# Expert blocks of 64 rows, two side by side on the halves of a product, in place of blocks of 128 rows

## The reference

```python
logits = flat @ router_w.T
scores = jax.nn.softmax(logits, axis=-1)
_, topk_idx = jax.lax.top_k(logits + router_bias, TOPK)          # TOPK = 2
...
for e in range(N_EXPERTS):                                       # 16
    h = jax.nn.silu(flat @ Wu[e]) * (flat @ Wg[e])               # 256 -> 128, twice
    out = out + combine[:, e:e + 1] * (h @ Wd[e])                # 128 -> 256
for s in range(N_SHARED):
    out = out + jax.nn.silu(flat @ Su[s]) * (flat @ Sg[s]) @ Sd[s]
...
x = x + jnp.tanh(g_ffn[0]) * _L0_ffn_ref(_layernorm(x, axis=-1), ...)
```

## Time and profile before

| | |
|---|---|
| median of 3 runs | 438.38 us (436.29 to 438.97) |
| the profiled execution's own time | 438.61 us |
| its span, first to last instruction | 436.8 us |
| mean granted clock of TensorE over the span | 0.969 of 2.4 GHz |
| PE busy over the span | 387.8 us (89%) |
| DVE / ACT / POOL busy | 352.9 / 294.6 / 278.0 us |
| blocks: first to last product of experts | about 369 to 418 us of the span |

### The profile page before, as it was taken

How to read it: one execution, slowest core, us unless ns; L and a number is a source line. 1 busy time by engine, 2 the same in 40 slices (tenths; PEclk the granted TensorE clock), 3 DMA queues, 4 the chain that set the end, 5 groups by cost and what they waited for, 6 DMA issues and landing times.

```text
span 436.8 us, 11224 instructions
## 1 busy us (share of the span) xinstructions
PE 387.8 (89%) x3626; PEld 288.6 (66%) x3626; DVE 352.9 (81%) x804; ACT 294.6 (67%) x621; POOL 278.0 (64%) x379
## 2 busy tenths in 40 slices
PE   0577799999999999999999999999998497999970
PEld 0445567667667767676766777676687286999960
DVE  5867979999999998999999999999889762334336
ACT  2598788777877777876877787787973315666510
POOL 2068866886787687688588677765574750366650
PEclk9999999999999999999999999999989688999995
DMA  8960868999980000000000000000194213444308
GB/s 209 261 228 2 106 90 259 253 287 286 243 230 3 0 0 0 0 0 0 0 0 0 0 0 0 0 2 2 33 434 194 96 67 98 124 132 136 99 22 277
DMA packets 34621, 45.57 MB, mean 104 GB/s; under 512 B 2970, under 2 KB 32031, under 8 KB 33696
## 3 DMA queue, kind: packets, MB, share of 16 engines
q1 hardware_dynamic: 26368, 35.34, 27.4%
q0 software_dynamic: 6944, 9.46, 9.9%
q10 hardware_dynamic: 1280, 0.41, 0.5%
HBM read 28.21 MB, written 24.19 MB: 120 GB/s over the span
## 4 chain that ended last, share of the span: by engine, by line
PE 73%; DVE 11%; ACT 4%; DMA 4%; issue 3%; POOL 3%; POOLq 0%; ACTq 0%; SPq 0%; DVEq 0%
PE proj_ps L972 18%; PE proj_ps L964 8%; PE score_ps L1001 8%; PE pv_ps L1024 8%; PE headT_ps L990 6%; PE out_ps L1034 6%; PE proj_ps L1138 4%; PE headT_ps L1138 3%; PE score_ps L990 3%; PE probT_ps L1010 3%; DMA cenf<-in_cen 2%; PE score_ps L1153 1%; DVE xs L1702 1%; DVE arena L1326 1%; PE pv_ps L1153 1%
## 5 line engine op out<-in xcount | busy, mean ns | idle before, releaser
L972 PE MATMUL proj_ps<-arena 128*128 128x512 f16 x384 | 100.0, 383 | 3.0 <-DVE arena L1356 3.0
L1364 DVE BATCH_NORM_STATS2 st<-rot 128x6 f32<-128x256 f32 x192 | 72.6, 419 | 10.6 <-ACT rot L710 10.0
L572 POOL TENSOR_TENSOR rot<-rot,cw 128x512 f32<-128x512 f32 x64 | 77.9, 1238 | 2.5
L710 ACT ACTIVATE rot<-proj_ps 128x512 f32<-128x512 f32 x96 | 56.1, 585 | 7.6 <-PE proj_ps L972 6.0
L972 PEld LDWEIGHTS proj_ps<-arena 128*128 (+1 forms) x384 | 32.5, 98 | 32.3 <-issue 3.8
L642 POOL DMA_INDIRECT ybuf<-arena,bslot x31 | 30.5, 984 | 31.3 <-DVE bslot L1612 14.6
L731 ACT ACTIVATE rot<-rot,cw 128x128 f32<-128x128 f32 x128 | 40.9, 391 | 11.0 <-POOL cw L566 10.4
L578 POOL TENSOR_TENSOR reg<-reg,rinv 128x512 f32<-128x512 f32 x32 | 33.4, 1044 | 21.9 <-DVE rinv L1374 21.9
L964 PE MATMUL proj_ps<-arena 128*128 128x512 f16 x192 | 46.7, 379 | 0.6 <-POOL arena L528 0.6
L1024 PEld LDWEIGHTS pv_ps<-reg,vv 64*128 64x128 f32 x512 | 31.1, 187 | 12.9 <-issue 9.7
L990 PE MATMUL headT_ps<-idf,rot 128*128 128x128 f32 x256 | 38.5, 273 | 0.1
(11 more groups left out here) (229 smaller groups left out, 850.2 us busy)
## 6 DMA issues: line engine op xcount, KB each, us to landing
zbuf<-fill SPq DMA_DIRECT2D x1, 16576.5 KB, 65.5
arena<-in_wffn SPq DMA_DIRECT2D x4, 1536.0 KB, 13.4
arena<-zbuf SPq DMA_DIRECT2D x30, 128.5 KB, 2.2
wkv_stage<-in_wkvN SPq DMA_DIRECT2D x1, 2048.0 KB, 15.4
wp_sb<-in_wpT POOLq DMA_DIRECT2D x1, 2048.0 KB, 16.4
wp_sb<-ybuf SPq DMA_DIRECT2D x8, 256.0 KB, 4.5
xs<-in_x SPq DMA_DIRECT2D x2, 512.0 KB, 5.5
vv<-in_wqN POOLq DMA_DIRECT2D x1, 1024.0 KB, 12.5
```

The lines of the kernel that those rows point to most:

```text
L572: gp.tensor_tensor(r, r, cw[:, 4 * i:4 * i + 4].unsqueeze(2).to_broadcast([P, 4, D]), ALU.mult)\
L710: act.activation(raw[c % 2][i], proj_ps[i % 2][:, :], ACT.Copy).then_inc(proj_evac, 1)
L972: mm = pe.matmul(ps, lhs, w[kind][:, ch, 512 * b:512 * b + 512], start=(k == 0), stop=(k == 3))
L1364: ins = ve.bn_stats(st[:, 4 * i + h:4 * i + h + 2, :].rearrange("p h s -> p (h s)"), raw[c % 2][i][:, h * D:(h + 2) * D].rearrange("p (h d ...
```

## The change

Blocks have 64 rows (`BR`). At most 47 exist; 48 are worked, four at a time in 12 steps: two in the lower 64 partitions of `zb`, two in the upper. In the product the 64 rows of tokens are stationary and occupy one half of the array's columns; 256 numbers of the weights move (up and gate side by side). The lower half takes its weights from `wall` at a register's place, the upper half takes them from a copy, `wfix`, that DVE and ACT make, one block each and all 768 numbers (three buffers, a wait on `down_done`). The result has the rows on the partitions, so the gated rows `hid` are transposed by PE (`hidden_transposes`, two more transposes), copied out by ACT (`hidden_out`), and are stationary for `block_down`, again in halves. SP reads four beginnings and issues four transfers of 64 rows for each step. POOL's scatters stay at 128 rows, two for each step. The table on DVE compares with 16 numbers for each expert instead of 8.

```diff
-NBLK = 31
-NPAIR = (NBLK + 1) // 2
+NBLK = 48
+NPAIR = NBLK // 4
...
-                for b in (range(1) if s == 0 else parts(s)):
-                    sp.dma_start(zb[s % 3][:, b, :], zbuf[bass.ds(base[b], P), :]).then_inc(zb_ld[s % 3], 16)
-                base = [sp.value_load(bbase[j:j + 1, 0:1], min_val=0, max_val=SLOTS)
-                        for j in range(2 * s + 2, min(2 * s + 4, NBLK))]
+                for j in range(2 if s == 0 else 4):
+                    half = slice(j % 2 * BR, (j % 2 + 1) * BR)
+                    sp.dma_start(zb[s % 3][half, j // 2, :], zbuf[bass.ds(base[j], BR), :]).then_inc(zb_ld[s % 3], 16)
+                if s + 1 < NPAIR:
+                    base = [sp.value_load(bbase[j:j + 1, 0:1], min_val=0, max_val=SLOTS)
+                            for j in range(4 * s + 4, 4 * s + 8)]
...
             def block_weights(s):
-                for b in parts(s):
-                    ins = act.activation(wup[s % 2][:, b, :], wall[:, bass.ds(base[b], 2 * H)], ACT.Copy)
+                if s >= 3:
+                    act.wait_ge(down_done, FIRST + s - 2)
+                act.activation(wfix[s % 3][:, 1, :], wall[:, bass.ds(base, WE)], ACT.Copy).then_inc(wfix_act, 1)
+            def hidden_out(s):
+                act.wait_ge(hidT_done, s + 1)
+                ge(act, down_done, FIRST + s - 1)
+                act.activation(hidT[s % 2], hidT_ps[s % 2][:, 0:2 * P].rearrange("p (b t) -> p b t", b=2),
+                               ACT.Copy).then_inc(hidT_evac, 1)
...
+            for s in range(NPAIR):
+                unit_silu(FIRST + s)
+                if s + 2 < NPAIR:
+                    block_rows(s + 2)
+                hidden_out(s)
+                if s + 2 < NPAIR:
+                    block_weights(s + 2)
...
+            def block_up(s, base):
...
+                for b in range(2):
+                    o = slice(b * 2 * P, (b + 1) * 2 * P)
+                    for c in range(HC):
+                        pe.matmul(up_ps[u % 2][0:BR, o], zTb[s % 2][:, b, c, 0:BR],
+                                  wall[:, bass.ds(base[b] + 2 * c * P, 2 * P)], start=(c == 0), stop=(c == HC - 1))
+                        mm = pe.matmul(up_ps[u % 2][BR:P, o], zTb[s % 2][:, b, c, BR:P],
+                                       wfix[s % 3][:, b, 2 * c * P:2 * (c + 1) * P], start=(c == 0), stop=(c == HC - 1))
+            def hidden_transposes(s):
+                pe.wait_ge(hid_done, u + 1)
+                ge(pe, hidT_evac, s - 1)
+                for b in range(2):
+                    mm = pe.transpose(hidT_ps[s % 2][:, b * P:(b + 1) * P], hid[u % 2][:, b * P:(b + 1) * P], idf[:, :])
...
-            for u in range(FIRST, end):
-                if u + 1 < end:
-                    bases[u + 1] = offsets(u + 1 - FIRST)
-                    block_up(u + 1)
-                if u - FIRST + 2 < NPAIR:
-                    block_transposes(u - FIRST + 2)
-                unit_down(u, bases[u])
+            block_up(0, base)
+            block_transposes(2)
+            hidden_transposes(0)
+            for s in range(NPAIR):
+                if s + 1 < NPAIR:
+                    following = offsets(s + 1)
+                    block_up(s + 1, following)
+                block_down(s, base)
+                base = following
+                if s + 3 < NPAIR:
+                    block_transposes(s + 3)
+                if s + 1 < NPAIR:
+                    hidden_transposes(s + 1)
...
+            def block_weights(s):
+                base = NSH * WE + ve.value_load(bbase[4 * s + 1:4 * s + 2, 1:2], min_val=0, max_val=(NE - 1) * WE)
+                if s >= 3:
+                    ve.wait_ge(down_done, FIRST + s - 2)
+                ve.tensor_copy(wfix[s % 3][:, 0, :], wall[:, bass.ds(base, WE)]).then_inc(wfix_dve, 1)
```

More of the change, by code:

```diff
@@ L102, in shared_tile, with scattered_back @@
     return u if u < FIRST else u - NPAIR if u >= FIRST + NPAIR else None
[L105 to L112, removed]
 def landed(s):
-    return 16 * sum(len(parts(r)) for r in range(s % 3, s + 1, 3))
+    return 64 * (s // 3 + 1)
+def scattered_back(s):
+    return 32 * (s // 3 + 1)
 def run_steps(eng, step, between={}):
@@ L265, in build @@
         zT = xT
-        wup = [qT[:, i, :, :].rearrange("p h t -> p (h t)").rearrange("p (b o) -> p b o", b=2) for i in range(2)]
+        hidT = [qT[:, i, 0:2, :] for i in range(2)]
+        wfix = [a[:, 0:2 * WE].rearrange("p (b o) -> p b o", b=2)
+                for a in (reg1, reg2, vv[:, :, :].rearrange("p a t -> p (a t)"))]
         yg = wp[:, :, :].rearrange("p h o -> p (h o)").bitcast(F32).rearrange("p (t k d) -> p t k d", t=NT, k=TOPK)
@@ L883, in _ @@
             act.wait_ge(table_done, 1)
[L884 removed]
+            base = [act.value_load(bbase[j:j + 1, 0:1], min_val=0, max_val=SLOTS) for j in (2, 3)]
             act.wait_ge(fill_done, 16)
             act.wait_ge(scattered, 16 * NT * TOPK)
[L887 removed]
+            for j in range(2):
+                act.dma_start(zb[0][j * BR:(j + 1) * BR, 1, :], zbuf[bass.ds(base[j], BR), :]).then_inc(zb_ld[0], 16)
             for i in range(1, 5):
                 act.wait_ge(ld_we[i], 16)
[L890 to L893, removed]
+            for s in range(2):
+                block_rows(s)
+                block_weights(s)
+            for s in range(NPAIR):
[5 more added lines that the diff above has]
+                    block_weights(s + 2)
+            for u in range(FIRST + NPAIR, NUNIT):
                 unit_silu(u)
[L895 to L897 removed]
         @block.tensor
@@ L1146, in unit_down @@
                     pe.wait_ge(y_done, NU * NT)
-                for b in parts_of(u):
+                for b in range(2):
                     h = hid[u % 2][:, b * P:(b + 1) * P]
[L1149 to L1154, removed]
+                    mm = pe.matmul(down_ps[u % 2][:, 0:H], h, wall[:, base[b] + 2 * H:base[b] + 3 * H],
+                                   start=(b == 0), stop=(b == 1))
                 mm.then_inc(down_done, 1)
@@ L1231, in _ @@
             pe.wait_ge(table_done, 1)
-            bases = {FIRST: offsets(0)}
+            base = offsets(0)
             for i in range(1, 5):
@@ L1487, in _ @@
             iota = rowv[:, NE:2 * NE]
-            full = rowv[:, 2 * NE:2 * NE + 8]
+            full = rowv[:, 2 * NE:2 * NE + NSTEP]
             block_no, block_row = rowv[:, NROWV - 2:NROWV - 1], rowv[:, NROWV - 1:NROWV]
@@ L1680, in _ @@
             route_weights()
-            unit_hidden(FIRST)
             unit_out(FIRST - 1)
             end = FIRST + NPAIR
-            row_places(0)
-            row_places(1)
-            for u in range(FIRST + 1, end - 1):
-                unit_out(u - 1)
-                unit_hidden(u)
-                row_places(u - FIRST + 1)
-            unit_hidden(end - 1)
-            unit_out(end - 2)
+            ve.wait_ge(table_done, 1)
+            for i in range(1, 5):
+                ve.wait_ge(ld_we[i], 16)
+            for s in range(2):
+                block_weights(s)
+                row_places(s)
+            for s in range(NPAIR):
+                unit_hidden(FIRST + s)
+                if s > 0:
+                    unit_out(FIRST + s - 1)
+                if s + 2 < NPAIR:
+                    block_weights(s + 2)
+                    row_places(s + 2)
             unit_out(end - 1)
```

85 lines of the change are left out of this document (48 added, 37 removed).

## The result

The changed kernel takes 455.97 us (median of 4 runs, 455.06 to 457.39), the kernel before beside it 437.71 (4 runs, 436.29 to 438.97): 1.0421 times as long, 95% interval 1.0376 to 1.0466, 18 us slower. The profiled execution took 456.06 us, its span is 454.2. The direction was predicted; 456 lies outside the range of 441 to 454, and the size was forecast at half of what it is.

A forecast was written before the change was run, and what follows sets the result against it. The prediction took PE's array as the bound before and its sequencer's loop, 4.63 us a step, after. The last scatter would land at 432.6 instead of 424.12, +8.5 on 438.6: 447 us, range 441 to 454.

The forecast's parts named there:

- SP's transfer: SP's queue in each step: 0.52 us for each of four transfers; with four loads, 4.3 us a step.
- the loop: PE's sequencer, from one up product's start to the next: offset loads queue behind the `hid` wait, 4.63 us a step.
- SP binds above the loop: Rival on SP's queue: its issues come slower, its step is 5.0 us, total 451 us; chance 0.15.
- The sign that the prediction gave for this rival: SP in the profile after: no wait behind its four transfers and four loads would mean SP is the bound, 451 us.
- Up(1) starts: Start of the blocks: after up(0) at 371.7 and hidden transposes at 374.8, the second up product starts at 376.5.
- if only in the first steps, 449: Rival on TensorE's clock: 1.2 GHz after idle gaps, only in the first steps, 449 us; all or part, chance 0.06.
- The tail: From the start of up(11) at 422.8 to the last scatter's landing at 432.6, with no POOL backlog.
- The halves: Expert products on PE: both array halves run at the same time, up 1.74 us and down 0.87 a step.
- the rival by which they show: Rival on PE's weight loads: not hidden under running products, 1.1 us a step, total 460 us; chance 0.02.
- A change of shape: PE's array, changing into halves and back: one such change a step, 0.14 us, giving 3.41 us of array time.
- DVE's copy: DVE's copy of 768 weights for the upper half: about 1.0 us, at the start ahead of up(0).
- the array rival: Rival with PE's array as bound: offset loads read ahead, cheaper SP transfers, steps of 3.41 us, total 433.5 us; chance 0.07.

The follow-up runs named there:

- e10_rows63: The changed kernel with blocks of 63 rows in place of 64: 449.92 us, 1.0259 times the kernel before.
- e5_before64: The kernel before with each transfer of 128 rows split into two of 64: 453.79 us, 1.0306 times the kernel before.
- e2_hoist: The changed kernel with PE's two offset loads moved ahead of the row transposes and the wait for `hid`: 455.21 us, 1.0341 times the kernel before.
- e1_static: The changed kernel with the 48 block beginnings written as constants, so SP does no register loads: 450.62 us, 1.0250 times the kernel before.
- e3_both: The changed kernel with the edits of e1_static and e2_hoist together: 438.10 us, 0.9962 times the kernel before.
- e9_before63: The kernel before with each transfer of 128 rows split into 63 and 65 rows: 446.17 us, 1.0172 times the kernel before.

## Why the prediction missed, step by step

**The step that failed is SP's transfer.** The prediction said: "A transfer of 64 rows may cost less to issue than one of 128; the bounds are 0 to 0.52". It cost more: 0.66 us from one to the next, where 0.52 was both my value and my upper bound. Four of them are 0.56 us over, and with four loads the turn is 4.94 instead of 4.3. Of the rest, up to the mean of 5.28, the chain shows single long instructions (a transfer of 1.06 at 409.23, loads of 0.45 to 0.52). That put SP above the loop of 4.5, and made the rival "SP binds above the loop" true, with a dearer step than its 5.0. Bounding the unknown from below alone was the error: the nearest row was one shape, and nothing in it excluded a higher price for another. The sign that the prediction gave for this rival, four loads with no wait behind them, is what the chain shows. That it is the issue time, and not the loads' count, is shown by e10_rows63, in which only the row count and so the issue time changes much: its ten steps from up(1) to up(11) take 425.23 - 379.81 = 45.4 us, where the kernel after needs 52.6. e5_before64 shows the same price in the other kernel.

**How the 8.8 us come about.** The last scatter has landed at 439.30 + 2.12 = 441.42, forecast 432.6.
- Up(1) starts at 378.50, forecast 376.5: +2.0. The granted clock was 0.50 of 2.4 GHz, its lower level, from 366 to 374; ahead of that PE had been busy for 0.93 us of the 2 from 362 to 364 and for none of the 2 from 364 to 366. The passes of up(0) lie 0.43 us apart instead of 0.217, 1.7 us in all. The prediction had this as a case, "if only in the first steps, 449".
- The loop: had all ten steps been as short as the quick ones, 4.53, they would make -1.0.
- The ten steps took 431.11 - 378.50 = 52.6 instead of 45.3: +7.3. The whole of it goes with SP's price, since e10_rows63 has none of it; but not all of it is SP's mean turn. 2.8 lie in one step (from 388.1 to 395.5), whose four transfers were issued from 387.04 to 389.50 and let the transposes start only at 393.62, 4.6 us after the start of the last issue (389.03) where 2.1 to 2.7 is usual. e2_hoist has its longest step, 6.90, at the same transfers (387.3 to 389.3), one of which took 4.0 us to land there, so this is no accident of one execution; why they land late isn't settled. Of the other steps those above the loop have 0.2 to 1.8 more each. In that with 1.8, up(9) began after an idle stretch at 420.20 and ran with passes 0.43 apart, 1.7 us for which the lower clock stands (0.55 granted from 420 to 422, after PE had been busy for 0.87 of the 2 us before) and SP only by having caused the gap.
- The tail: 10.3 instead of 9.8, +0.5. Here the prediction had a term at nothing: "POOL has 2.6 us of scatters in 4.6 us and no backlog". Behind up(11) the down products of the last two steps follow each other in 2.1 us, and the last four scatters start at 435.43, 436.72, 438.01 and 439.30, one behind the other. The last result was ready at 436.82; with 0.77 to its first scatter, as before, that would be at 437.6, and it is at 438.01.

So of the 8.8 us about 3.4 are passes at the lower clock (1.7 in up(0), 1.7 in up(9)), which the prediction had given 0.06 as a case of its own.

From there to the end of the span it is 12.8 us, as before.

**The loop on PE's sequencer** was right in its mechanism and its size: 2.83 from the start of up to the end of `hid` (395.46 to 398.29), as forecast, and 1.71 to the next up where 1.8 was, 4.54 against 4.63. The prediction gives the lower end of its 447 once as 442.8 and once as 444.7; only the second follows from its bounds. e1_static and e10_rows63 show it alone, in every step, and e2_hoist takes it away by moving nothing but two loads. In the changed kernel it costs little by itself, since SP is later.

**The halves.** They pair, as the earlier trace rows had it: records of the two halves start 10 ns apart and the pairs 0.215 us, in the timeline of up(1):

```profile
378.77 0.38 PE L1203 MATMUL headT_ps<-arena 128*64 x1
378.78 0.38 PE L1205 MATMUL headT_ps<-reg,arena 128*64 128x256 f32 x1
378.98 0.38 PE L1203 MATMUL headT_ps<-arena 128*64 x1
378.99 0.38 PE L1205 MATMUL headT_ps<-reg,arena 128*64 128x256 f32 x1
```

Their weights are hidden: the two loads of a pair, 0.14 us each and 10 ns apart, lie within its 0.215. So the rival by which they show doesn't hold, and the rule of the Trainium skill ("TensorE: Matmul & The Clock Gate", Part 3) on which it stood, that a load overlaps running products only where the row group differs, is contradicted here too, for two column groups on the same rows. (The same part also names the background weight buffer as a case in which a load runs ahead, which the prediction left out.) A change of shape costs 0.15 us (the row transposes 0.59 instead of 0.44, the first up pass 0.36 instead of 0.21), twice a step; the prediction had one of 0.14. The array's step is therefore 3.55, not 3.41. The Trainium skill (TensorEngine Tiling (Array Packing), Key Properties) has a change of tiling mode drain the engine. The trace agrees, with 0.15 us for each change; that it is a drain is the page's word, not the trace's.

**DVE's copy** of 768 numbers takes 0.56 us, forecast "about 1.0". It was not on the path.

**Why the freed version doesn't win.** e3_both has what the array rival asked for, steps of 3.55, but its time of 433.5 isn't reached. From the first to the last product of experts it takes 45.0 us (371.12 to 416.14) where the kernel before takes 48.7 (369.24 to 417.96): ten steps are 35.2, but the first, with up(0) at the lower clock, is 4.9, and the last up product with what must follow it is 4.9 more. The products start 1.9 us later than before, behind a wider table, two transfers and a copy of weights. From the last product to the last landing it is 5.4 us instead of 6.2, and that end is POOL's: the last four scatters start at 415.56, 416.85, 418.14 and 419.43, one behind the other, and the chain leaves PE at 414.07, with the down products of the last step but one. 3.7 and 0.8 less 1.9 is the 2.6 us by which its last scatter lands earlier; of these 1.4 are in the medians (438.10 beside 439.47).

## What to carry to other kernels

Halving a tile doubles the instructions on every queue that feeds it: count each queue's turn for a step, SP's and PE's sequencer among them, before the array's, and let the price of a shape that the trace doesn't show go up as well as down. When two bounds lie close together, an edit against one shows only part of what both cost, here 0.8 or 1.7 of 4.6 points; try both at once before dropping either. Where the list of waits names a releaser that ended earlier than the wait did, look at the waiting engine's own sequencer.

## What the hardware did that I had not expected

- The issue of a DMA with exactly 64 rows occupied SP for 0.466 us; with 8 to 128 rows, in sixteen other counts, 0.25 to 0.33. It was the same for 257 and 256 numbers and for both halves of the partitions, and 0.597 for the second of two with nothing between them. What makes 64 special stays open.
- The first register load on SP behind transfers of 63 or 65 rows took 0.53 us or more in every step (e9_before63, e10_rows63), once 1.09; behind transfers of 64 or 128 rows it took 0.27 to 0.30. What lengthens it stays open.
